# A tile's weight load ordered ahead of the step's two loads of spread rows, on SyncE's queue (a Mamba block and a mixture of experts in one kernel)

## The reference

```
def mamba(x):                      # per sequence, width d = 256, state 16
    x_ssm, x_gate = split(x @ in_proj_w.T + in_proj_b)
    x_conv = silu(causal_conv(x_ssm, 4 taps))
    B, C   = split(x_conv @ bc_w.T + bc_b)         # 16 rows each
    dt     = softplus(x_conv @ dt_w.T + dt_b)
    for t: h = h * exp(dt[t] * A) + dt[t] * B[t] * x_conv[t];  y[t] = sum_n h * C[t] + x_conv[t] * D
    return layernorm((y * silu(x_gate)) @ out_w.T + out_b + x)
def moe(x):                        # 8 experts, hidden 1024, the best 2 for each token
    w = softmax over the two largest of silu(x @ rw1 + rb1) @ rw2 + rb2
    return x + sum_e w[e] * (silu(x @ we1[e] + be1[e]) @ we2[e] + be2[e])
```

## Time and profile before

| what | us |
|---|---|
| median of 3 runs | 930.38 (929.67 to 933.92) |
| the profiled execution, its own time | 937.38 |
| its span on the core | 935.0 |
| DVE busy in the span | 781.6 |
| PE busy in the span | 790.0 |
| ACT busy in the span | 664.7 |
| POOL busy in the span | 601.8 |
| mean granted share of TensorE's full clock | 0.954 |

### The profile page before, as it was taken

The page is one execution under the profiler, slowest core; times in us unless marked ns, Lnnn a source line. Parts: engine busy times, 40 slices in busy tenths (PEclk is TensorE's granted clock), DMA queues, the critical chain, the costliest instruction groups (busy, mean ns, idle before and its releaser), DMA issues.

```text
span 935.0 us, 14382 instructions
## 1 busy us (share of the span) xinstructions
PE 790.0 (84%) x4533; PEld 639.3 (68%) x4533; DVE 781.6 (84%) x774; ACT 664.7 (71%) x1134; POOL 601.8 (64%) x384
## 2 busy tenths in 40 slices
PE   3994859898998899889988998989988998899852
PEld 2662648777776778677866887677767786778741
DVE  6818857997989988997899699969898789969993
ACT  1433677858688778876887779686887788769930
POOL 3571525676478747774777756785687487758861
PEclk9996979998999999989999999999999999999985
DMA  9939446577657876787579775776588667877741
GB/s 298 388 142 343 178 135 222 184 222 226 185 181 220 254 224 204 218 249 217 187 209 260 240 221 176 234 260 197 168 222 281 189 216 205 252 214 235 230 90 22
DMA packets 81927, 201.00 MB, mean 215 GB/s; under 512 B 7936, under 2 KB 41216, under 8 KB 81728
## 3 DMA queue, kind: packets, MB, share of 16 engines
q1 hardware_dynamic: 61424, 171.46, 53.9%
q0 software_dynamic: 19168, 26.59, 15.0%
q10 hardware_dynamic: 1264, 2.05, 0.7%
HBM read 174.38 MB, written 26.61 MB: 215 GB/s over the span
## 4 chain that ended last, share of the span: by engine, by line
PE 32%; DVE 31%; issue 9%; ACT 9%; DMA 8%; SPq 2%; POOL 1%; DVEq 0%; ACTq 0%; POOLq 0%
PE ps_up L1248 14%; DVE ps_drive L954 11%; PE ps_yx L1262 8%; DVE ring L961 8%; DVE ps_drive L947 6%; DMA bc_scratch<-sp 6%; PE ps_fr L1179 4%; ACT L805 3%; DVE xx L928 2%; ACT da L778 2%; PE ps_up L1242 2%; DMA out<-yo,sid 2%; PE ps_fr L1204 1%; SPq L527 1%; DMA xg<-xn_scratch,gid 1%
## 5 line engine op out<-in xcount | busy, mean ns | idle before, releaser
L598 POOL TENSOR_TENSOR y<-y,ring 128x1024 f32<-128x1024 f32 x126 | 326.2, 2589 | 61.6 <-ACT y L769 54.2
L954 DVE TENSOR_TENSOR_SCAN ps_drive<-da,ps_drive 128x1024 f32<-128x1024 f32 x128 | 293.7, 2295 | 57.8 <-ACT da L778 54.2
L1248 PEld LDWEIGHTS ps_up<-xgt,w1s 128*128 128x128 f32 x2272 | 290.9, 200 | 18.8 <-issue 9.6
L1248 PE MATMUL ps_up<-xgt,w1s 128*128 128x128 f32 x2272 | 290.3, 283 | 0.0
L1262 PE MATMUL ps_yx<-w,ht 128*128 x1136 | 270.6, 381 | 0.0
L1262 PEld LDWEIGHTS ps_yx<-w,ht 128*128 128x128 f32 x1136 | 206.4, 191 | 28.7 <-issue 5.0
L587 POOL DMA_INDIRECT out<-yo,sid x71 | 115.6, 1628 | 145.1 <-ACT yo L820 98.2
L805 ACT ACT_TABLE_LOAD x143 | 183.5, 1283 | 2.5
L778 ACT ACTIVATE da<-gd,col 128x511 f32<-128x511 f32 x256 | 168.3, 710 | 0.0
L947 DVE TENSOR_TENSOR ps_drive<-ps_u,rep 128x1024 f32<-128x1024 f32 x128 | 157.4, 1229 | 9.5 <-DVE ring L961 0.5
L961 DVE TENSOR_TENSOR ring<-ps_drive,rep 128x1024 f32<-128x1024 f32 x128 | 156.5, 1223 | 3.9
(11 more groups left out here) (172 smaller groups left out, 720.4 us busy)
## 6 DMA issues: line engine op xcount, KB each, us to landing
w1s<-in_we SPq DMA_DIRECT2D x71, 1024.0 KB, 7.3
rep<-bc_scratch SPq DMA_DIRECT2D x128, 512.0 KB, 4.7
w<-in_we SPq DMA_DIRECT2D x8, 1024.0 KB, 12.0
w<-in_x SPq DMA_DIRECT2D x8, 512.0 KB, 11.1
xn_scratch<-da SPq DMA_DIRECT2D x8, 512.0 KB, 7.0
out<-w POOLq DMA_DIRECT2D x8, 512.0 KB, 6.4
xnt_scratch<-xx SPq DMA_DIRECT2D x8, 512.0 KB, 5.9
xx<-xnt_scratch SPq DMA_DIRECT2D x8, 512.0 KB, 3.5
```

The costliest lines, as they stand in the source:

```text
L598: pool.tensor_tensor(y[:, :, :], y[:, :, :], ring[:, g % RING, :, :], ALU.add).then_inc(s_sum, 1)
L954: dve.tensor_tensor_scan(states, da[:, g % DECAYS, :, :].rearrange("p k l -> p (k l)"), states, 0.0, ALU.mult, ALU.add).then_inc(s_scanned, 1)
L1248: mm = pe.matmul(bank[:, c * P:(c + 1) * P], w1s[:, q, k, at:at + P], xgt[:, k, :], start=False, stop=(c == 3 and k == KD - 1))
```

## The change

On SyncE, in each of the 72 steps, `load_w1` is called ahead of the step's two `load_rep`, and not behind them. Nothing else is changed; the waits inside the two functions are the same.

```
@@ -558,12 +558,12 @@
                     for i in range(STEPS):
                         if i == 1 and b < B - 1:
                             load_xnt(b + 1)
+                        if b * STEPS + i + WBUF < MT:
+                            load_w1(b + (i + WBUF) // STEPS, (i + WBUF) % STEPS)
                         for r in range(NU if i < IN else 0):
                             g = b * NST + i * NU + r + REPS
                             if g < B * NST:
                                 load_rep(g)
-                        if b * STEPS + i + WBUF < MT:
-                            load_w1(b + (i + WBUF) // STEPS, (i + WBUF) % STEPS)
                         if i == 5 and b < B - 1:
                             store_bc(b + 1)
                         if i == 7 and b > 0:
```

## The result

The changed kernel took 923.59 us (median of 22 runs, 918.37 to 932.63), the kernel before 931.74 (22 runs, 929.16 to 937.84) on the same chips. The ratio is 0.9903, 95% interval 0.9884 to 0.9921: 1.0% faster, where 2.3% were forecast. (The ratio leaves out one run of the changed kernel, 932.63, taken in a slower state of the chip.) 923.59 lies 2.6 us above the range.

A forecast was written before the change was run, and what follows sets the result against it. A batch's DVE part and ACT/PE part, joined by the bc_scratch store, bound the kernel. Seven store-to-scan stretches fall from 198.79 to 177.1 us, a gain of 21.7: 930.4 - 21.7 = 908.7 us, range 898 to 921.

The forecast's parts named there:

- The store: SyncE, step 5: store issued 2.2 us sooner, landing 6.4 after issue; ACT resumes 2.8 sooner, yo starts 2.2 sooner.
- Early w1 worth nothing of its own: Step 5: PE's 1.48 us idle for w1 goes, but is no gain of its own, as DVE bounds that stretch.
- To the first scan: From yo to the next batch's first scan 16.2 us instead of 17.7; first scan 3.7 us sooner.
- The base: Profiled execution 7.0 us above the runs' median; the 21.7 us gain summed there is taken off the median 930.4.
- What follows shifts with it: After the first scan: PE's chain up to 463.65, then DVE, start sooner too, with no loss counted.
- rival D: Slower, chance 0.05: step 1's rep load, behind x^T and w1, 0.3 to 2.5 us late; covered by DVE's 2.96 idle.
- a wait of DVE for rep at unit 5, seven times: Sign in the profile, at unit 5 of a batch, listed as showing the forecast wrong; no size given.
- B: Next batch's start, chance 0.13: something just behind limits it, only 1 to 2 us a batch arrive; 916 to 925.7 us.
- C: Before 463.65, chance 0.08: freed time returns as a wait elsewhere, DVE's 2.96 idle grows by the gain; 930 us.
- A: At yo, chance 0.08: the scatter-add is no limit and all of ACT's store wait goes; 896 us.
- worst case for the store, 922: Store lands in 8.0 us, clock unchanged: ACT resumes 1.2 sooner in seven batches, a gain of 8 us.

The follow-up runs named there:

- e1: Changed kernel with step 1 alone in the old order (x^T, rep, rep, w1): 920.80 us, ratio to before 0.9864.
- e2: Kernel before with only the store moved ahead of its step's w1 load: 917.79 us, ratio to before 0.9852.
- e4: Changed kernel with the store put back behind step 6's w1 load: 936.63 us, ratio to before 1.0024.
- e6: Changed kernel with step 1 in the old order and two yo buffers: 910.62 us, ratio to before 0.9754.
- e7: Kernel before with the store ahead of its step's w1 load and two yo buffers: 916.17 us, ratio to before 0.9810.
- e8: Kernel before, unchanged, run and profiled a second time: median 933.54 us, ratio 0.9993; profiled execution 931.80 us.
- e3: Kernel before with step 1 alone in the new order (x^T, w1, rep, rep): 937.91 us, ratio to before 1.0040.
- e10: Changed kernel with step 1's x^T load moved behind that step's two rep loads: 923.52 us, ratio to before 0.9907.

## Why the prediction was wrong in size and right in direction

*The store.* Right in kind. It went 0.4 after the start of the rep load (forecast: 0.1 after its end), and in the batch that was worked out it landed in 5.2 for 6.4; over the main stage it took 3.7 to 7.9 us, wider than the forecast 4.5 to 6.6. ACT's wait for it fell to 7.1 and in the second profile to 3.8 (forecast: under 4). `yo` became the next limit at the scatter-add.

*Early w1 worth nothing of its own.* Right for this kernel, by e1, e2 and e4; with two `yo` it is worth 5.5 us (e6 and e7).

*To the first scan.* About right in the pair of profiles, 22.6 for 21.7. In the batch that was worked out it was 31.59 - 28.98 = 2.6 for 3.7: `yo` came 5.7 after the resume for a forecast of 4.8, and from `yo` to the scan it took 17.56 at a clock of 0.94, not 16.2 at 1.00. DVE's idle there is 5.09, not 2 to 3.

*The base.* The gain was summed in one execution and taken off the median. That execution was 7.0 above the median, and the prediction knew it but took the gain whole. e8 shows the 5.5 us between two executions in exactly these stretches. Against it the gain of this part is 16.7, so 5.0 of the error of 14.9 us stand here, and 1.4 are the median of more runs (931.74 for 930.38).

*What follows shifts with it.* This is the step that failed: "What follows (PE's chain up to 463.65, then DVE) shifts with it, as both sides start sooner", and with it the price of rival D, "That is covered, as DVE idles 2.96 right behind". D had the lateness about right: 0.3 to 2.5 forecast, 2.16 in the batch shown, 1.0 to 3.8 in the seven (three of them over 2.5); it called a wait of DVE for rep at unit 5, seven times, a sign against itself, and that is what came. The cover held too, in every batch, the first with 3.76 included. What D left out is who else was in the burst: POOL's scatter-add, through it ACT's `yo` and POOL's sum, and through that DVE. The sign was in the earlier trace rows, where L928 takes 1.85 us; beside its 0.76 elsewhere the hold by POOL shows. The cost in DVE's part is 6.0 us in one profile and 8.9 in the other, of which by e3 and e10 some 2 to 3 come back in the part with the store (for e10 195.8 us there for 193.1 and 193.5). With 8.9, 5.0 and 1.4, less 1.2 in the rest of the span, 14.1 of the 14.9 us are accounted for. The experiments say the same without any profile: the store alone gains 14 to 16 us (e2, by ratio and by medians), the whole change 8 to 9, where 21.7 were forecast. So 6 to 8 us of the forecast gain were never there, and 5 to 7.5 were there and were lost to the early w1 loads, 3.7 to 4.5 of them to step 1's (e3). The rest, up to 3 us, is the difference of e1 and e2, and lies inside their intervals.

*The rivals.* The time is that of B, but for another reason than B gave: the gain did arrive behind the store, and it was partly lost some 33 us into the next batch's scans. The measured 923.59 also lies above the prediction's own worst case for the store, 922, since that case held nothing for what the early w1 loads might cost. C is out: the freed time didn't come back as a wait before 463.65. A is out, since `yo` does wait. That the scatter-add is a limit worth 10 us on the changed kernel, and little on e2, stands in no part of the prediction.

## What to carry to other kernels

When a load is moved, list every transfer that is in flight with it, on all queues, and not only the one behind it in its own queue: here the load of the same queue was late at no cost, and the timelines put the cost on a scatter-add from another engine's queue. An idle that is to cover a delay must be checked to its end: look at the instruction behind the idle, and if it takes longer than its like, something else ends it. And a sum over stretches of one execution wants a second execution before it is taken off a median, above all if the first lies above it.

## What the hardware did that was not expected

A 0.5 MB load issued 1.6 us behind 0.5 MB and 0.5 us behind 1 MB of the same queue landed after 9.6 us (up to 10.4 in the main stage; the median of all rep loads is 4.7), and a scatter-add of POOL's queue, issued 0.7 after the burst's first load, took 8.6 where it took 5.0. A DVE instruction of 0.76 us lasted 3.12 beside a POOL sum of 2.35, and no row of the profile names POOL as what held it. A store that follows a 0.5 MB load landed after 3.7 to 7.9 us, where behind a 1 MB load it took 6.9 to 8.0.
